# Moving the row statistics of x1 from VectorE to ScalarE and GpSimd, with a new order of one step, in a cross-attention and feed-forward kernel

## The chip, the cores and the metric

The kernel runs on one core of a Trainium2 chip. The metric is the device time of one execution in microseconds (us). A core has five engines that run their own instruction queues in order and meet only through semaphores: TensorE (PE; PEld is its weight loading), VectorE (DVE), ScalarE (ACT), GpSimd (POOL), and SyncE (SP), which here only issues transfers.

## What is computed

For 64 blocks x[b] of 256 rows by 256, each with a context of 120 rows by 192:

```
x  = x + softmax(q kT / sqrt(32)) v @ Wo + bo      q = layernorm(x) @ Wq, k = ctx @ Wk, v = ctx @ Wv, 8 heads
h  = layernorm(layernorm(x), g1, b1)               (x is now x1)
h  = quant(h) @ ternary(w1) + b1                   256 -> 1024
h  = quant(layernorm(gelu(h), g2, b2))
x  = x + h @ ternary(w2) + b2                      1024 -> 256
```

`quant` scales each row by 127 / max|row| and rounds. The two layernorms in front of w1 are folded into one: with mean m and variance v of a row of x1, h = (x1 - m) * g1 * r + b1, with r = (v * (1 + eps) + eps^2) ^ -0.5.

## The kernel before

The work has two stages. In the first, the attention of all 64 blocks runs as a software pipeline; its result x1 and the quantised rows `hq` of the feed-forward input are made there too. In the second, the feed-forward runs over the 64 blocks. The change lies in the first stage.

One step i of the first stage is the function `attn(i, n)`, which each engine has in a version of its own; its order is written out by hand. Steps 28 to 58 run in a hardware loop unrolled by 4; those before and after are written out. In step i, block i has its scores and exponentials, block i-1 its values and sums, block i-2 its output projection and x1, block i-3 its quantisation, block i+2 its queries and keys, and block i+4 the statistics of x. The names that matter:

- TensorE (L1340): `scores` (raw scores, matmul L1249), `values` (o, L1276), `sums` (L1285), two tiles of `project` (y, L1331), `turn_minima` between them (L1256), `first_values`, `shift` (adds the negated maximum to the scores, L1262), `keys` (L1300 to L1305), `queries` (L1321), `spread_inverses` (L1312).
- VectorE (L692), in this order: `affine` of h (i-3; L700), `largest` (maximum of the scores, into nm_part; L689), h_max (L711), nm_row (L716), h_cl (L721), nm_t (L727), addition of x1 (L733), h_qs (L737), inv_sum (L742), bn_stats of x1 (L747), inv_part (L755), bn_aggr (L760), centring of h (L765) with f_ve between its two halves (L769), q_t (L777), o_t (L786). `shift` waits for nm_t, inv_part for ScalarE's inv_hi.
- ScalarE (L1005): copies of keys and values (L1001, L1003), of o (`copy_o`, L984), the statistics of x by two sums and two squares (L1016, L1020), two exponentials (L995), inv_hi (L989), two more exponentials, `cast_rows` (L979).
- GpSimd (L514): add_b2 (i-3), add_bo (i-1), the r chain of block i+3 (three small operations), `quantise` (i-3), and the power f_r (i-2; L541), which `affine` of the next step needs.
- SP (L384) issues each step's transfers, the store and the reload of r (L378, L416) among them, which it waits for in its queue. Weights are loaded one piece a step from step 4 on; eight steps have a wide weight operation on ScalarE (L970 in steps 12 to 15, L962 in steps 20, 22, 24 and 26), behind the body of the step.

PSUM has 8 banks: bank 0 holds sums and spread, bank 1 o and the turned minima nm_p, bank 2 keys and y, banks 2 and 3 queries and values' projection, banks 4 to 7 the scores. `keys` waits for x1's addition, since that reads y out of bank 2.

## Time and profile before

| | |
|---|---|
| median of 3 runs | 1152.22 us (1152.06 to 1157.33) |
| the profiled execution | 1157.24 us, its span 1155.6 us |
| busy: TensorE, VectorE, ScalarE, GpSimd | 984.1, 1070.7, 815.4, 711.5 us |
| share of the span | 85%, 93%, 71%, 62% |
| granted TensorE clock, mean | 0.98 |
| first stage | to some 660 us, 64 steps |
| second stage | from some 690 us |

Times in the rows count from the span's start. An engine's timeline gives start and length of each instruction; neighbours on one engine may overlap by a little, so that the distance of two starts, not the length, is what an instruction costs its engine. In brackets stands how long the engine stood idle ahead of an instruction, and which one released it.

### The profile page before, as it was taken

What the parts mean: (1) busy time and instruction counts of PE and PEld (TensorE: products, weight loads), DVE (VectorE), ACT (ScalarE), POOL (GpSimd) and SP (SyncE); (2) the same over time, 40 slices, a digit from 0 to 9 for tenths busy, and PEclk for the clock granted to TensorE, in tenths of its full rate; (3) what the DMA queues carried; (4) which work ended last, traced back from release to release, by engine and by line L of the source; (5) the groups of instructions that cost most, each with busy time, mean ns of one, the idle gap of its engine ahead of it and who ended that gap; (6) DMA issues with size and microseconds to landing.
All of it is one profiled execution on the core that took longest, in us unless ns stands there. A gap on an engine that the chain in (4) does not pass through costs nothing.

```text
span 1155.6 us, 29367 instructions
## 1 busy us (share of the span) xinstructions
PE 984.1 (85%) x9649; PEld 655.4 (57%) x9649; DVE 1070.7 (93%) x1711; ACT 815.4 (71%) x2091; POOL 711.5 (62%) x930
## 2 busy tenths in 40 slices
PE   5999998999999999999999767887777777777775
PEld 3666666666666666666666433544444444444444
DVE  2799988999999999999999899999999999999997
ACT  3655565566655566556654476999999999999993
POOL 3355555666555555555556436777777777777776
PEclk8999999999999999999999888999999999999998
DMA  4677956666767667776765301333233333323334
GB/s 142 137 159 161 165 125 159 147 148 146 149 152 148 152 144 156 150 150 141 150 149 122 97 19 23 38 37 37 35 38 36 36 36 36 37 36 36 36 36 72
DMA packets 145430, 114.71 MB, mean 99 GB/s; under 512 B 52536, under 2 KB 135864, under 8 KB 145360
## 3 DMA queue, kind: packets, MB, share of 16 engines
q1 hardware_dynamic: 127776, 96.90, 38.4%
q0 software_dynamic: 16864, 16.26, 11.9%
q8 instruction: 40, 0.66, 0.3%
q10 hardware_dynamic: 720, 0.66, 0.2%
q14 instruction: 30, 0.25, 0.1%
HBM read 71.75 MB, written 33.63 MB: 91 GB/s over the span
## 4 chain that ended last, share of the span: by engine, by line
DVE 43%; issue 25%; PE 21%; DMA 6%; SPq 3%; POOL 1%; DVEq 1%; ACT 1%; POOLq 0%; ACTq 0%
DVE nm_part L689 10%; PE banks L1321 9%; DVE gn_low L813 7%; DVE gn_high L813 7%; DMA r_rows<-x_r 5%; PE banks L1300 3%; DVE xr L733 3%; DVE h L700 3%; DVE o_t L786 2%; PE banks L1331 2%; DVE gn_low L799 2%; DVE gn_high L799 2%; PE banks L1302 1%; DVE h_max L711 1%; DVE g_max L819 1%
## 5 line engine op out<-in xcount | busy, mean ns | idle before, releaser
L995 ACT ACTIVATE probs<-banks 120x512 f32<-120x512 f32 x256 | 138.4, 596 | 110.6 <-PE banks L1262 110.5
L689 DVE TRANSPOSE_TENSOR_REDUCE nm_part<-banks 128x64 f16<-128x2048 f32 x64 | 147.8, 2309 | 3.7 <-PE banks L1249 3.7
L1033 ACT ACTIVATE g_dev<-g,g_sum 128x1024 bf16<-128x1024 f32 x128 | 149.1, 1165 | 0.0
L1038 ACT ACTIVATE g<-banks,h_dq 128x1024 f32<-128x1024 f32 x128 | 142.4, 1130 | 8.1 <-PE banks L1196 8.1
L502 POOL TENSOR_TENSOR xr<-xr,b_bc 128x512 f32<-128x512 f32 x64 | 82.6, 1290 | 102.2 <-DVE h L700 100.4
L1331 PE MATMUL banks<-wo_sb,o_t 128*128 128x256 f32 x512 | 140.8, 398 | 1.1 <-DVE o_t L847 1.0
L1214 PE MATMUL banks<-w_t,g_t 128*128 128x256 bf16 x1008 | 125.3, 279 | 14.5 <-ACT g_t L1071 11.9
L1190 PE MATMUL banks<-w_t,h_t 128*128 128x512 bf16 x512 | 127.7, 394 | 2.0 <-ACT g L1038 1.3
L1321 PE MATMUL banks<-xt,wq_c 128*128 128x256 f32 x512 | 128.3, 393 | 0.0
L1214 PEld LDWEIGHTS banks<-w_t,g_t 128*128 128x128 f16 x1008 | 95.8, 100 | 54.1 <-issue 26.8
L574 POOL TENSOR_TENSOR g_r<-g_ve,neg_half 128x2 f32<-128x2 f32 x64 | 104.5, 1633 | 8.6 <-ACT g_ve L1054 8.6
L541 POOL TENSOR_TENSOR f_r<-f_ve,neg_half 128x2 f32<-128x2 f32 x62 | 49.6, 801 | 92.2 <-DVE f_ve L769 92.2
L497 POOL TENSOR_TENSOR xr<-xr,bo_bc 128x512 f32<-128x512 f32 x64 | 81.1, 1266 | 39.3 <-DMA xr<-in_x 39.1
L1321 PEld LDWEIGHTS banks<-xt,wq_c 128*128 128x128 f32 x512 | 92.5, 190 | 17.9 <-issue 0.2
L1331 PEld LDWEIGHTS banks<-wo_sb,o_t 128*128 128x128 f32 x512 | 86.9, 189 | 21.0 <-issue 14.1
L549 POOL TENSOR_TENSOR g_dq<-g_max,w_out 128x2 f32<-128x2 f32 x64 | 12.6, 197 | 131.0 <-DVE gn_low L813 70.5
L1001 ACT ACTIVATE k_t<-banks 128x256 f32<-128x256 f32 x64 | 24.5, 383 | 91.4 <-DVE q_t L777 91.2
L1208 PE MATMUL banks<-ident_h,gn_low 128*128 128x128 f16 x512 | 40.3, 223 | 51.6 <-POOL gn_low L554 51.6
L799 DVE SCALAR_TENSOR_TENSOR gn_high<-g,g_nm,g_bc 128x1024 f32<-128x1024 f32 x64 | 80.9, 1271 | 0.0
L799 DVE SCALAR_TENSOR_TENSOR gn_low<-g,g_nm,g_bc 128x1024 f32<-128x1024 f32 x64 | 80.9, 1271 | 0.0
L813 DVE SCALAR_TENSOR_TENSOR gn_low<-gn_low,g_r,b2n_bc 128x1024 f32<-128x1024 f32 x64 | 79.2, 1279 | 0.0
L1249 PE MATMUL banks<-q_t,k_t 32*128 32x256 f32 x1024 | 75.0, 407 | 4.9 <-ACT k_t L1001 4.8
(167 smaller groups left out, 2599.2 us busy)
## 6 DMA issues: line engine op xcount, KB each, us to landing
x_in<-in_x SPq DMA_DIRECT2D x64, 256.0 KB, 4.6
xt<-in_x_t SPq DMA_DIRECT2D x64, 256.0 KB, 4.2
xr<-in_x SPq DMA_DIRECT2D x64, 256.0 KB, 5.4
out<-xr SPq DMA_DIRECT2D x64, 256.0 KB, 5.9
out<-res POOLq DMA_DIRECT2D x62, 256.0 KB, 4.4
ctx_t<-in_ctx_t SPq DMA_DIRECT2D x64, 128.0 KB, 3.9
r_bc<-r_rows SPq DMA_DIRECT2D x64, 128.0 KB, 4.6
w_raw<-in_w_t SPq DMA_DIRECT2D x8, 256.0 KB, 5.2
```

Source lines behind the costliest of these rows:

```text
L502: pool.tensor_tensor(xr[:, r, :, :], xr[:, r, :, :], b2_bc[:, :].unsqueeze(1).to_broadcast([P, T, D]), ALU.add).then_inc(b2_done, 1)
L574: pool.tensor_tensor(g_r[:, q, :], g_ve[:, q, :], neg_half[:, 0:T], ALU.pow).then_inc(gr_done, 1)
L689: dve.tensor_reduce(nm_part[:, :, 0:C * RB], blocks_p, AX.X, ALU.max, negate=True, apply_transpose=True).then_inc(max_done, 1)
L799: dve.scalar_tensor_tensor(out=gn[n][:, t, :], in0=g[:, p, t, :], scalar=g_nm[:, p, t:t + 1], in1=g2_bc[:, :], op0=ALU.add, op1=ALU.mult). ...
L813: dve.scalar_tensor_tensor(out=gn[n][:, t, :], in0=gn[n][:, t, :], scalar=g_r[:, p, t:t + 1], in1=b2n_bc[:, :], op0=ALU.mult, op1=ALU.add) ...
L995: act.activation(probs[:, p, j, :, :], sc_p[0:KV, j, :, :], ACT.Exp, scale=SCALE).then_inc(probs_done, 1)
L1033: act.activation(g_dev[:, t, :], g[:, p, t, :], ACT.Square, scale=-float(F), bias=g_sum[:, p, t:t + 1], accum_out=g_ssq[:, p, t:t + 1]).th ...
L1038: act.activation(g[:, p, t, :], u_p[t], ACT.Gelu, scale=h_dq[:, b, t:t + 1], accum_out=g_sum[:, p, t:t + 1]).then_inc(gelu_done, 1)
L1190: pe.matmul(u_p[t][:, cols], h_t[:, b, t * C + c, :], w1_t[:, c, cols], start=(c == 0), stop=False, skip_group_check=True)
L1214: pe.matmul(y[t], turned_rows[:, t, f, :], w2_t[:, f, :], start=(first and f == 0), stop=False, skip_group_check=True)
L1321: last = pe.matmul(q_p[:, m, :], wq_c[:, c, m * P:(m + 1) * P], xt[:, p, c, :], start=(c == 0), stop=(c == C - 1))
L1331: last = pe.matmul(y_p[:, t, :], o_t[:, p, c, t * P:(t + 1) * P], wo_sb[:, c, :], start=(c == 0), stop=(c == C - 1))
```

## The change

- VectorE: `largest` comes first in the step. The centring of h moves one step later (block i-3 in place of i-2) and stands behind `largest`; nm_row and nm_t follow, then `affine`, h_max, the addition of x1, h_cl, h_qs, inv_sum, inv_part, q_t, o_t. bn_stats, bn_aggr and f_ve are gone for the blocks up to 61; the last two keep them.
- ScalarE: `row_statistics(i-2)`, two sums (as means) and two squares, stands at the end of the step; `cast_rows` moves ahead of the statistics of x.
- GpSimd: `scale_rows(i-3)` makes f_ve by two small operations and f_r by the power, first in the step; then the r chain, `quantise`, then add_b2 (behind a wait for inv_part) and add_bo.
- TensorE: y moves to bank 1 (`project` waits for copy_o, `values` for x1's addition of the step before), the turned minima to bank 0 (no wait for copy_o). `keys` no longer waits for x1; its short matmuls come first.
- SP: the output's store one step later and ahead of the r store; the reload of r ahead of the load of xr.

```diff
-        y_p = bank[2].rearrange("p (t n) -> p t n", t=T)
+        y_p = bank[1].rearrange("p (t n) -> p t n", t=T)
-        nmt_p = bank[1][:, 0:P // 2].bitcast(F16)
+        nmt_p = bank[0][:, P:P + P // 2].bitcast(F16)
...
+                def scale_rows(b, m):
+                    after(pool, h_affine, b - 1)
+                    pool.wait_ge(x1_ssq, b * T + T)
+                    pool.tensor_tensor(f_ve[:, m, :], f_ssq[:, m, :], var_mul[:, :], ALU.mult).then_inc(f_ve_done, 1)
+                    pool.wait_ge(f_ve_done, 2 * b + 1)
+                    pool.tensor_tensor(f_ve[:, m, :], f_ve[:, m, :], var_add[:, :], ALU.add).then_inc(f_ve_done, 1)
+                    pool.wait_ge(f_ve_done, 2 * b + 2)
+                    pool.tensor_tensor(f_r[:, m, :], f_ve[:, m, :], neg_half[:, 0:T], ALU.pow).then_inc(f_r_done, 1)
...
-                        pool.wait_ge(h_affine, b + 1)
-                        add_b2(b, (n + 1) % 4)
-                    b = i - 1
-                    if live(b, NB):
-                        add_bo(b, (n + 3) % 4)
+                        scale_rows(b, q)
...
+                    b = i - 3
+                    if live(b, NB):
+                        pool.wait_ge(split_done, i)
+                        add_b2(b, (n + 1) % 4)
+                    b = i - 1
+                    if live(b, NB):
+                        add_bo(b, (n + 3) % 4)
...
+                    if isinstance(i, int) and i == -1:
+                        largest(0)
+                    elif live(i, NB) and not (isinstance(i, int) and i == 0):
+                        largest(i)
+                    b = i - 3
+                    if live(b, NB):
+                        after(dve, hq_cast, b - 3)
+                        dve.wait_ge(x1_ssq, b * T + T)
+                        for t in range(T):
+                            last = dve.scalar_tensor_tensor(out=h[:, r1, t, :], in0=xr[:, r1, t, :],
+                                                            scalar=f_mean[:, q, t:t + 1], in1=g1_bc[:, :],
+                                                            op0=ALU.subtract, op1=ALU.mult)
+                        last.then_inc(h_centred, 1)
...
+                def row_statistics(b, p, r):
+                    after(act, f_ve_done, 2 * b - 2)
+                    after(act, h_centred, b - 1)
+                    act.wait_ge(x1_done, b + 1)
+                    for t in range(T):
+                        act.activation(x1_sq[:, p, t, :], xr[:, r, t, :], ACT.Copy, scale=1.0 / D,
+                                       accum_out=f_mean[:, p, t:t + 1]).then_inc(x1_summed, 1)
+                    for t in range(T):
+                        act.wait_ge(x1_summed, b * T + t + 1)
+                        act.activation(x1_sq[:, p, t, :], xr[:, r, t, :], ACT.Square, scale=-1.0,
+                                       bias=f_mean[:, p, t:t + 1], accum_out=f_ssq[:, p, t:t + 1]).then_inc(x1_ssq, 1)
...
-                    if live(i - 4, NB):
-                        cast_rows(i - 4, n % 4)
+                    if live(i - 2, NB):
+                        row_statistics(i - 2, p, (n + 2) % 4)
...
-                    pe.wait_ge(min_done, b + 1)
+                    after(pe, x1_done, b - 1)
...
-                    after(pe, x1_done, b - 3)
+                    after(pe, k_done, b)
...
-                        pe.wait_ge(q_done, left(b + 4))
-                        pe.wait_ge(k_done, left(b + 4))
+                        pe.wait_ge(o_done, left(b + 2))
                         pe.wait_ge(on_done, b + 1)
```

## Rows read from the trace of the kernel before

**Rows 1.** Windows: stretch; busy PE, PEld, DVE, ACT, POOL; clock, DMA share, GB/s.

```profile
300.00:580.00 280.00, 270.10 (x3014) 192.66 (x3017) 265.82 (x577) 166.11 (x484) 160.73 (x258) 1.00 0.70 149
```

**Rows 2.** Timeline, VectorE, one step: start, length, engine, line, operation.

```profile
443.20 2.31 DVE L689 TRANSPOSE_TENSOR_REDUCE nm_part<-banks 128x64 f16<-128x2048 f32 x1
...
445.43 0.64 DVE L711 TENSOR_REDUCE h_max<-h 128x2 f32<-128x512 f32 x1
...
446.90 0.69 DVE L733 TENSOR_TENSOR xr<-banks,xr 128x512 f32<-128x512 f32 x1
...
447.58 0.94 DVE L742 RECIPROCAL inv_sum<-banks 128x128 f32<-128x128 f32 x1
...
448.43 0.69 DVE L747 BATCH_NORM_STATS2 f_st<-xr 128x6 f32<-128x256 f32 x2
...
449.25 0.35 DVE L755 SCALAR_TENSOR_TENSOR inv_part<-inv_hi,part_sign,inv_sum 128x128 f16<-128x128 f16 x1
...
452.95 2.31 DVE L689 TRANSPOSE_TENSOR_REDUCE nm_part<-banks 128x64 f16<-128x2048 f32 x1
```

**Rows 3.** Timeline of the same step, TensorE and ScalarE.

```profile
441.32 1.15 PE L1249 MATMUL banks<-q_t,k_t 32*128 32x256 f32 x16
...
442.01 0.38 ACT L1001 ACTIVATE k_t<-banks 128x256 f32<-128x256 f32 x1 [1.32 <-DVE q_t L777]
...
443.60 0.60 ACT L984 ACTIVATE o_raw<-banks 128x512 f32<-128x512 f32 x1 [0.92 <-PE banks L1276]
...
444.27 1.13 PE L1331 MATMUL banks<-wo_sb,o_t 128*128 128x256 f32 x4
```

**Rows 4.** Timeline of the first steps, TensorE and VectorE.

```profile
31.95 1.15 PE L1249 MATMUL banks<-q_t,k_t 32*128 32x256 f32 x16
...
33.24 2.32 DVE L689 TRANSPOSE_TENSOR_REDUCE nm_part<-banks 128x64 f16<-128x2048 f32 x1 [0.39 <-PE banks L1249]
...
43.54 1.13 PE L1331 MATMUL banks<-wo_sb,o_t 128*128 128x256 f32 x4
...
44.76 0.29 DVE L716 TENSOR_REDUCE nm_row<-banks 128x32 f16<-128x128 f16 x1 [0.54 <-PE banks L1256]
...
45.16 0.42 DVE L727 TENSOR_TENSOR nm_t<-nm_row,block_sel 128x256 f16<-128x256 f16 x1
```

**Rows 5.** Timeline behind the loop, VectorE.

```profile
680.58 0.48 DVE L877 SCALAR_TENSOR_TENSOR h<-h,f_r,b1n_bc 128x256 f32<-128x256 f32 x1
...
681.49 0.69 DVE L882 TENSOR_REDUCE h_max<-h 128x2 f32<-128x512 f32 x1
```

**Rows 6.** Timeline of step 62, VectorE and ScalarE.

```profile
644.69 0.94 DVE L742 RECIPROCAL inv_sum<-banks 128x128 f32<-128x128 f32 x1
...
645.72 0.31 ACT L989 ACTIVATE inv_hi<-inv_sum 128x128 f16<-128x128 f32 x1 [0.16 <-DVE inv_sum L742]
646.09 1.09 ACT L995 ACTIVATE probs<-banks 120x512 f32<-120x512 f32 x2
```

**Rows 7.** Timeline of step 15, ScalarE and TensorE's weight loads.

```profile
181.41 0.30 ACT L989 ACTIVATE inv_hi<-inv_sum 128x128 f16<-128x128 f32 x1
181.61 1.07 ACT L995 ACTIVATE probs<-banks 120x512 f32<-120x512 f32 x2
...
182.74 0.74 PEld L1249 LDWEIGHTS banks<-q_t,k_t 32*128 32x128 f32 x16 [0.30 <-ACT probs L995]
```

**Rows 8.** Timeline, ScalarE: first and last instruction of one block's statistics of x.

```profile
444.09 0.41 ACT L1016 ACTIVATE x_sq<-x_in 128x256 bf16<-128x256 f32 x1
...
445.78 0.19 ACT L1020 ACTIVATION_READ_ACCUMULATOR x_sq<-x_in,x_sum 128x1 f32 x1
```

**Rows 9.** Groups by line, GpSimd: busy us, mean ns | idle before.

```profile
L541 POOL TENSOR_TENSOR f_r<-f_ve,neg_half 128x2 f32<-128x2 f32 x62 | 49.6, 801 | 92.2 <-DVE f_ve L769 92.2
```

**Rows 10.** Timeline, ScalarE: a weight operation of step 15.

```profile
183.09 1.06 ACT L970 ACTIVATE w_t<-w_raw 128x1024 bf16<-128x1024 f32 x1
```

**Rows 11.** SP's queue, 80 to 190 us: waits in total, times, longest.

```profile
SPq L416 <- DMA r_rows<-x_r: 52.0, 11, 6.7
```

More of the change, by code:

```diff
@@ L536, in attn @@
                         weight_steps[i]()
-                    b = i - 2
+                    b = i - 3
                     if live(b, NB):
-                        after(pool, h_affine, b - 1)
-                        pool.wait_ge(f_ve_done, b + 1)
-                        pool.tensor_tensor(f_r[:, p, :], f_ve[:, p, :], neg_half[:, 0:T], ALU.pow).then_inc(f_r_done, 1)
+                        pool.wait_ge(split_done, i)
[3 more added lines that the diff above has]
+                        add_bo(b, (n + 3) % 4)
                 def store(b, r):
@@ L694, in attn @@
                     r1, r2 = (n + 1) % 4, (n + 2) % 4
+                    if isinstance(i, int) and i == -1:
[3 more added lines that the diff above has]
+                    b = i - 3
+                    if live(b, NB):
+                        after(dve, hq_cast, b - 3)
[5 more added lines that the diff above has]
+                        last.then_inc(h_centred, 1)
+                    b = i
+                    if live(b, NB):
+                        dve.wait_ge(nmt_ps, b + 1)
+                        dve.tensor_reduce(nm_row[:, :], nmt_p.rearrange("p (k r) -> p r k", r=32), AX.X, ALU.min).then_inc(min_done, 1)
+                        after(dve, sc_ps, b)
+                        dve.wait_ge(min_done, b + 1)
+                        dve.tensor_tensor(nm_t[:, :, :], nm_row[:, :].unsqueeze(1).to_broadcast([P, RB, 32]),
+                                          block_sel[:, :].unsqueeze(2).to_broadcast([P, RB, 32]), ALU.mult).then_inc(nmt_done, 1)
                     b = i - 3
@@ L703, in attn @@
                         last.then_inc(h_affine, 1)
-                    if isinstance(i, int) and i == -1:
-                        largest(0)
-                    elif live(i, NB) and not (isinstance(i, int) and i == 0):
-                        largest(i)
                     b = i - 3
@@ L735, in attn @@
                     if live(b, NB):
+                        after(dve, hq_done, b - 1)
+                        dve.wait_ge(h_maxed, b + 1)
+                        dve.tensor_scalar(h_cl[:, q, :], h_max[:, q, :], CLIP, 1.0 / QMAX,
+                                          ALU.max, ALU.mult).then_inc(h_clipped, 1)
                         dve.wait_ge(h_clipped, b + 1)
@@ L742, in attn @@
                         dve.reciprocal(inv_sum[:, q, :], sum_p).then_inc(inv_done, 1)
-                    b = i - 2
-                    if live(b, NB):
-                        dve.wait_ge(x1_done, b + 1)
-                        for t in range(T):
-                            last = dve.bn_stats(f_st[:, p, t, :], xr[:, r2, t, :])
-                        last.then_inc(x1_stats, 1)
                     b = i - 1
@@ L891, in _ @@
                 steps(dve, A0, NB, L0, L1, attn, 4, aside)
+                dve.wait_ge(x1_ssq, (NB - 2) * T)
+                centre_h(NB - 3, 1, [f_mean[:, 1, t:t + 1] for t in range(T)])
                 affine_h(NB - 3, 1)
@@ L899, in _ @@
                 statistics(NB - 2, 2)
-                centre_h(NB - 2, 2)
+                centre_h(NB - 2, 2, [f_mv[:, 0, t, 0:1] for t in range(T)])
                 ffn(0, 0, True)
@@ L906, in _ @@
                 statistics(NB - 1, 3)
-                centre_h(NB - 1, 3)
+                centre_h(NB - 1, 3, [f_mv[:, 1, t, 0:1] for t in range(T)])
                 ffn(2, 2)
```

94 lines of the change are left out of this document (36 added, 58 removed).

## The prediction, made before the changed kernel ran

> **What bounds the kernel now.** Read the sum by stage first: between 300 and 580 us VectorE is busy 265.8 of 280 us, TensorE 270.1, ScalarE 166.1, GpSimd 160.7, at granted clock 1.00 [rows 1]. Two engines are near full, so no share decides; the order of one step does. The timeline of VectorE has one block of attention per 9.75 us: `largest` starts at 443.20 and again at 452.95, and nothing stands idle between [rows 2]. TensorE begins the scores of this step at 441.32 [rows 3], 1.88 us before `largest`: VectorE first finishes `o_t` and then the normalisation's second half, `affine`, of an older block. The loop that closes is `largest` -> transposition of the minima -> second output tile -> addition of x1 -> keys -> queries -> `q_t`, `o_t`, `affine` -> `largest`. TensorE waits in it twice, for the minima and for x1, because y shares bank 2 with the keys. By its idle time (9.9 of 280 us, over 28.7 steps) TensorE alone would need about 9.4 us.
>
> **What is taken away.** From VectorE, for each of 62 blocks: bn_stats (start to next start 448.43 to 449.25, 0.82 us) [rows 2], and with it bn_aggr and f_ve, which together are shorter (by the rows' distances I put all three at 1.2 us; the sum below doesn't use it). y moves to bank 1, so the keys no longer wait for x1. `largest` stands ahead of `affine`. If only this counted, VectorE would fall to some 8.5 us and TensorE's 9.4 would set the step.
>
> **The new chain.** Let the scores of block i start at 0. I follow VectorE's new order to the next scores. A self-wait is a wait of an engine for its own last result.
> - Scores to `largest`: 1.29 (31.95 to 33.24, a place where VectorE was free) [rows 4].
> - `largest`: 2.23 (443.20 to 445.43) [rows 2]. Sum 3.52. The two centring instructions now stand here, 0.40 each by the two `affine` instructions, of the same kind and size (680.58 to 680.98 is one) [rows 5]: 4.32. The transposition is done by then (below).
> - nm_row to nm_t with its self-wait: 0.40 (44.76 to 45.16) [rows 4]: 4.72. nm_t is 0.42 long [rows 4]; a neighbour without a self-wait starts 0.08 to 0.09 before the end (inv_sum, 0.94 long, has its next at 0.85 [rows 2]): 0.34, sum 5.06.
> - `affine` twice, then the self-wait for h_max: 0.91 (680.58 to 681.49) [rows 5]: 5.97.
> - h_max, 0.64 long [rows 2], the same overlap: 0.56, sum 6.53. Adding x1 and h_qs before the reciprocal of the sums: 0.68 (446.90 to 447.58) [rows 2]. h_cl now stands between with a self-wait, 0.20 (0.16 of its own and a gap like those above): 7.41.
> - The reciprocal `inv_sum` to ScalarE's inv_hi: 1.03 (644.69 to 645.72) [rows 6]: 8.44. Nothing of VectorE's lies between `inv_sum` and this any more, and ScalarE has long run its first two exponentials.
> - inv_hi to the third exponential: 0.20 (181.41 to 181.61) [rows 7] or 0.37 (645.72 to 646.09, where ScalarE had waited for `inv_sum` as it will here) [rows 6].
> - Third and fourth exponential to the next scores: 1.13 (181.61 to 182.74), where TensorE is shown to wait for exactly this [rows 7].
>
> Sum: 9.77 to 9.94 us, against 9.75. So the step hardly changes: the exponentials stand in ScalarE's queue behind inv_hi, inv_hi behind `inv_sum`, and `inv_sum` now behind centring and `affine`, which before lay partly on the other side of it. I take 9.86, the middle, since both ends are rows of the same operations: +0.11.
>
> The Trainium skill speaks against three of these terms. Its page "VectorE: DVE Perf Modes", section "The DRAIN you can't avoid", says that the pipe empties between two Vector instructions anyway and that a semaphore between them costs nothing extra. By that the self-waits would vanish and the period would not exceed the old one. The rows here disagree: instructions without such a wait overlap by 0.09 us (inv_sum, as above) [rows 2], and with it 0.40 passes for a nm_row of 0.29 [rows 4].
>
> **Does the rest stay hidden?** ScalarE gains two sums and two squares per block. The same four cost 1.88 us at 444.09 to the last accumulator read's end at 445.97 [rows 8]. They start when the last exponential ends, about 0.15 before the next scores, end at +1.7; the copies of keys and values (0.38 each, overlapping by 0.1) end by 2.4, and copy_o, which starts at +2.28 today (443.60 against 441.32) and takes 0.60 [rows 3], ends at 2.9. `project`'s first tile starts at +2.95 now (444.27) [rows 3] and in the new kernel waits for copy_o, since y takes o's bank. From that tile to nm_row 1.22 us pass (43.54 to 44.76, where only the transposition lies between) [rows 4]: 4.17, against 4.32 on VectorE. Covered, by 0.15 to 0.2 us only. ScalarE's total rises to 8.2 us, under 9.8. GpSimd: two small operations and the power, which takes 0.80 [rows 9]; were all three as long, 2.4 from +1.9, so by 4.3, and `affine` asks for it at 5.06. Its r chain of block i+3 follows, of the same three kinds; SP's r store waits for that, and the reload of r has a whole step before use. add_b2 and add_bo come behind inv_part and run beside q_t, o_t and `largest`; x1's addition asks for add_bo only at 6.5 of the next step. Each covered. TensorE's own work arrives at the scores after 9.4 at the latest, and the other path from inv_hi, over inv_part (0.35 long [rows 2]) and the four short spread matmuls, is shorter than the 1.33 through the exponentials.
>
> **Places where it isn't hidden.** Eight steps (12 to 15, and every second from 20) put a wide weight operation into ScalarE's queue behind the new statistics: 1.06 long [rows 10]. It then stands ahead of copy_o, where the cover was 0.2: up to +1.0 each, 8 us. In steps 80 to 190 us SP stands 52 us for r_rows in eleven steps, up to 6.7 [rows 11], while weights load, and steps are longer than 9.85 already; the later x loads and the output ahead of the r store shift this by -3 to +6. Four of the eight steps fall there and their delay partly lies beside that one. I take +4.5 for both. In the unrolled steps, where a step takes 9.85 today, +0.05 of 20 steps: 1.0. The loop of 31 steps: 31 x 0.11 = 3.4. At the end ScalarE has the statistics (1.88) in front of the first bias copy and lost the cast (0.5) there: +1.4.
>
> Sum: 3.4 + 1.0 + 4.5 + 1.4 = 10.3 us. The profiled execution took 1157.24 (span 1155.6), so its like would take 1167.5. That execution lies 5.0 above the median 1152.22, so the median forecast is 1162.5, +0.9%.
>
> **Rivals.**
> 1. *ScalarE's queue costs more* (chance 0.25): 9.95 in the loop (31 x 0.20 = 6.2), 0.15 in 20 unrolled steps (3), all eight weight steps at full price (8), SP's order +4, tail 1.4: +22.6, 1175. For it: the 0.37 row is the one with ScalarE waiting. Against: one row only.
> 2. *The weight steps cost nothing, since they fall beside the transfers* (0.24): 3.4 + 1.0 + 1.4, 1158 or a little less, within 0.5%. A measurement of this kernel can tell about 0.5% from no change, 1146.5 to 1158.
> 3. *TensorE becomes the bound, faster* (0.18): the place is the semaphore waits and the exponentials' start. If the chain above is shorter than 9.4, the step is TensorE's 9.4: -0.35 x 31 and -0.45 x 25, +4 for the rest, 1134. It decides from 0.4 us: for instance, were the three self-waits free (0.20 + 0.11 + 0.05 to 0.13) and inv_hi read earlier. The rule of the Trainium skill cited above gives this same outcome. Against it: the waits show in rows 4 and 5.
> 4. *The change doesn't take hold*: the last two blocks still use bn_stats, but 62 of 64 change, so no chance of its own.
>
> **How the numbers follow.** Forecast 1162.5 with 1158 to 1169: chance 0.33. Slower still 0.25, same 0.24, faster 0.18. Slower by over 0.5%: 0.33 + 0.25 = 0.58. The range leaves out the lower end of rival 3 and the far end of rival 1: 1143 to 1180.
>
> **What would show it.** Right: VectorE idle ahead of `largest` (for the scores) by 0.5 us or more and ahead of inv_part (for inv_hi) by 0.4 in each step; the scores' weight loads waiting for probs; VectorE's busy time in attention down by about 70 us; ScalarE idle some 1.4 us ahead of inv_hi; steps near 9.86. Wrong: steps near 9.4 with TensorE never waiting (rival 3), or the first output tile waiting for o_raw in each step (ScalarE's cover of 0.2 was gone), or f_r or xr late, which would put GpSimd on the path.

## The result, and the profile after

The changed kernel takes 1199.58 us (median, 1197.96 to 1202.08) beside 1154.49 us for the kernel before on the same chip: ratio 1.040, 95% interval 1.0375 to 1.042. The prediction said 1162.5 and 1143 to 1180. The sign was right, the size far off and outside the range.

The profiled execution took 1198.2 us, its span 1196.4. First the busy times over the whole span, from the page:

```profile
PE 977.5 (82%) x9603; PEld 645.7 (54%) x9649; DVE 1025.4 (86%) x1401; ACT 926.1 (77%) x2587; POOL 731.2 (61%) x1056
```

VectorE fell by 45.3 us and ScalarE rose by 110.7, as meant. Now the same window as [rows 1], with the same columns:

```profile
300.00:580.00 280.00, 251.51 (x2799) 174.06 (x2801) 226.20 (x402) 204.74 (x673) 156.01 (x292) 1.00 0.53 137
```

TensorE is busy for 251.5 of 280 us in place of 270.1, VectorE for 226.2 in place of 265.8, and the DMA share fell from 0.70 to 0.53. The two engines that were near full no longer are, and ScalarE is at 204.7 of 280, so something else sets the step. Nearly the whole loss lies in the first stage: from the first `largest` to the last of the 64 pass 628.3 us before (21.6 to 649.9) and 666.2 after (21.3 to 687.5), +37.9 of the +40.8 in the span; 3.25 are behind the last `largest`.

The view that names the culprit is the waits of SP's own queue, 300 to 620 us (total, times, longest):

```profile
SPq L420 <- DMA r_rows<-x_r: 154.2, 31, 6.8
```

SP stands for five of the some ten microseconds of each step in front of the reload of r (r_bc), until its own store of r (r_rows) has landed, that is, until the semaphore that tells of its end has come. For the kernel before, the same view has two rows:

```profile
SPq L416 <- DMA r_rows<-x_r: 80.7, 33, 3.7
SPq L378 <- POOL x_r L531: 60.8, 33, 4.4
```

The second row is the important one, because it is gone afterwards. Before, SP came to the store early and waited for GpSimd's x_r: it had slack in every step. After, it never waits there; x_r has been ready for some time when SP comes. SP's timeline of one step after the change (issue instructions, start and length):

```profile
478.06 0.37 SPq L386 DMA_DIRECT2D r_rows<-x_r  x1
483.63 0.37 SPq L420 DMA_DIRECT2D r_bc<-r_rows  x1
484.28 0.41 SPq L424 DMA_DIRECT2D xr<-in_x  x1
484.85 1.20 SPq L390 DMA_TRANSPOSE h_t<-hq  x1
486.23 0.45 SPq L400 DMA_DIRECT2D ctx_t<-in_ctx_t  x1
486.77 0.38 SPq L402 DMA_DIRECT2D xt<-in_x_t  x1
487.42 0.38 SPq L406 DMA_DIRECT2D x_in<-in_x  x1
487.99 0.41 SPq L410 DMA_DIRECT2D out<-xr  x1
488.58 0.37 SPq L386 DMA_DIRECT2D r_rows<-x_r  x1
493.87 0.37 SPq L420 DMA_DIRECT2D r_bc<-r_rows  x1
...
499.25 0.37 SPq L386 DMA_DIRECT2D r_rows<-x_r  x1
```

The store is issued at 478.06, its landing lets the reload go at 483.63 (5.6 us), and then seven issues stand in a row until the next store at 488.58 (4.95 us). The next round is 5.3 + 5.4. In these rounds the loop passes no compute engine: SP's queue shows no wait for one. It takes 10.5 to 10.7 us, and everything else follows. The chain of work, followed back through 480 to 503 us, says the same; its first entry is

```profile
478.06 5.55 DMA r_rows<-x_r
```

and the landing of r_rows is on that chain again from 488.58 (5.27) and from 499.25. Its users see it on VectorE's timeline; `q_t` waits for the reload, and `largest` starts 10.15 us apart here:

```profile
487.32 0.69 DVE L776 TENSOR_TENSOR q_t<-banks,r_bc 128x512 f32<-128x512 f32 x1 [1.50 <-DMA r_bc<-r_rows]
...
488.53 2.31 DVE L706 TRANSPOSE_TENSOR_REDUCE nm_part<-banks 128x64 f16<-128x2048 f32 x1
...
498.68 2.32 DVE L706 TRANSPOSE_TENSOR_REDUCE nm_part<-banks 128x64 f16<-128x2048 f32 x1 [0.27 <-PE banks L1266]
```

Earlier, before weights are loaded, the steps are the predicted ones:

```profile
59.73 2.32 DVE L706 TRANSPOSE_TENSOR_REDUCE nm_part<-banks 128x64 f16<-128x2048 f32 x1 [0.57 <-PE banks L1266]
...
69.50 2.32 DVE L706 TRANSPOSE_TENSOR_REDUCE nm_part<-banks 128x64 f16<-128x2048 f32 x1 [0.57 <-PE banks L1266]
```

That is 9.77 us. So the engines' chain and SP's loop are two loops of similar length, and the longer one sets the step.

How far from this was the kernel before? SP's timeline of the step of [rows 2]:

```profile
444.97 0.38 SPq L398 DMA_DIRECT2D x_in<-in_x  x1
447.53 0.36 SPq L378 DMA_DIRECT2D r_rows<-x_r  x1
448.07 0.38 SPq L408 DMA_DIRECT2D xr<-in_x  x1
448.67 0.41 SPq L412 DMA_DIRECT2D out<-xr  x1
451.58 0.35 SPq L416 DMA_DIRECT2D r_bc<-r_rows  x1
...
454.67 0.38 SPq L398 DMA_DIRECT2D x_in<-in_x  x1
```

From store to reload pass 4.05 us, with the load of xr and the output's store issued *while* it lands; from the reload to the end of x_in's issue 3.5. That is a loop of some 7.5 us in a step of 9.75, with 2.2 us of slack, which is the wait for x_r between 445.35 and 447.53. The change moved two issues (1.15 us) out of the landing's shadow, and put a 256 KB store right ahead of the 1 KB one. With the old landing that would have been 4.05 + 5.4 = 9.45 us at most, still hidden under 9.77. But the median landing in 300 to 620 us rose from 4.0 to 5.5 us (the list of DMA issues), and 5.5 with 4.95 to 5.4 of issues makes 10.45 to 10.9. By this sum the loss needed both, the moved issues and the longer landing; what made the landing longer stays open (last section).

### The profile page after: what moved, and what is told of

It is laid out like the page before. It is cut to its first block, busy times and chain, and to the rows that moved or that the text cites. A ratio compares the mean times of both kernels' runs of the same rounds, so it can differ in the third digit from the quotient of the medians.

```text
span 1196.4 us, 29791 instructions
## 1 busy us (share of the span) xinstructions
PE 977.5 (82%) x9603; PEld 645.7 (54%) x9649; DVE 1025.4 (86%) x1401; ACT 926.1 (77%) x2587; POOL 731.2 (61%) x1056
## 4 chain that ended last, share of the span: by engine, by line
DMA 26%; DVE 25%; issue 24%; SPq 16%; PE 4%; POOL 2%; ACT 2%; DVEq 1%; ACTq 0%; POOLq 0%
DMA r_rows<-x_r 24%; DVE gn_low L812 7%; DVE gn_high L812 6%; SPq L390 5%; DVE gn_low L798 2%; SPq L410 2%; DMA r_bc<-r_rows 2%; SPq L400 2%; DVE gn_high L798 2%; SPq L424 2%; SPq L406 2%; DVE nm_part L706 2%; SPq L402 2%; SPq L420 1%; DVE g_max L818 1%
## 5 line engine op out<-in xcount | busy, mean ns | idle before, releaser
L706 DVE TRANSPOSE_TENSOR_REDUCE nm_part<-banks 128x64 f16<-128x2048 f32 x64 | 147.7, 2308 | 11.2 <-PE banks L1266 10.7
L1229 PE MATMUL banks<-w_t,g_t 128*128 128x256 bf16 x1008 | 123.7, 277 | 10.4 <-ACT g_t L1086 7.7
L517 POOL COPY h_dq<-h_cl 128x2 f32<-128x2 f32 (+1 forms) x64 | 13.7, 214 | 185.9 <-DVE h_qs L759 184.8
L1205 PE MATMUL banks<-w_t,h_t 128*128 128x512 bf16 x466 | 117.5, 389 | 6.2 <-ACT bias_st L1074 2.4
L1337 PE MATMUL banks<-xt,wq_c 128*128 128x256 f32 x512 | 121.4, 380 | 0.0
L776 DVE TENSOR_TENSOR q_t<-banks,r_bc 128x512 f32<-128x512 f32 x64 | 44.3, 692 | 80.0 <-DMA r_bc<-r_rows 64.3
L1031 ACT ACTIVATE x_sq<-x_in 128x256 bf16<-128x256 f32 x128 | 52.1, 408 | 67.2 <-DMA x_in<-in_x 64.1
L1346 PEld LDWEIGHTS banks<-wo_sb,o_t 128*128 128x128 f32 x512 | 88.6, 193 | 28.5 <-ACT o_raw L997 13.9
L565 POOL TENSOR_TENSOR g_dq<-g_max,w_out 128x2 f32<-128x2 f32 x64 | 12.1, 189 | 131.2 <-DVE gn_low L812 70.7
L1223 PE MATMUL banks<-ident_h,gn_low 128*128 128x128 f16 x512 | 40.8, 224 | 54.2 <-POOL gn_low L570 54.2
L1266 PE MATMUL banks<-q_t,k_t 32*128 32x256 f32 x1024 | 75.0, 408 | 12.2 <-ACT k_t L1014 4.9
L1002 ACT ACTIVATE inv_hi<-inv_sum 128x128 f16<-128x128 f32 x64 | 19.8, 309 | 80.9 <-DVE inv_sum L764 80.7
```

Source lines behind the costliest of these rows:

```text
L706: dve.tensor_reduce(nm_part[:, :, 0:C * RB], blocks_p, AX.X, ALU.max, negate=True, apply_transpose=True).then_inc(max_done, 1)
L1205: pe.matmul(u_p[t][:, cols], h_t[:, b, t * C + c, :], w1_t[:, c, cols], start=(c == 0), stop=False, skip_group_check=True)
L1229: pe.matmul(y[t], turned_rows[:, t, f, :], w2_t[:, f, :], start=(first and f == 0), stop=False, skip_group_check=True)
L1337: last = pe.matmul(q_p[:, m, :], wq_c[:, c, m * P:(m + 1) * P], xt[:, p, c, :], start=(c == 0), stop=(c == C - 1))
L1346: last = pe.matmul(y_p[:, t, :], o_t[:, p, c, t * P:(t + 1) * P], wo_sb[:, c, :], start=(c == 0), stop=(c == C - 1))
```

## The experiments

**Theory A**: SP's loop (landing plus the issues behind the reload) sets the step; beneath it lies the engines' chain of 9.77 to 9.94 that the prediction worked out. **Theory B**: the engines' new order itself costs more, through ScalarE or VectorE, and SP's waiting is only a follower. Ratios are to the kernel before, timed beside each. "In the loop" are the steps from 28 on, of the profiled execution; each profile has some longer steps besides.

| kernel | ratio, 95% interval | span | steps (starts of `largest`) |
|---|---|---|---|
| changed | 1.040 [1.0375, 1.042] | 1196.4 | 9.78 to 11.6 in the loop, mean 10.5 |
| e1, store of r ahead of output | 1.0228 [1.0191, 1.0264] | 1180.5 | 9.77 to 11.1 in the loop, one of 12.2, mean 10.2 |
| e2, reload one step later | 1.017 [1.0147, 1.0192] | 1168.9 | 9.78 and 9.89 in the loop, and two of 11.6 and 12.3 |
| e8, issues behind the store | 1.016 [1.0101, 1.0219] | 1178.5 | 9.78 to 9.92 in the loop, one of 10.1 |
| e3, old engines, SP's new order | 1.0695 [1.0666, 1.0724] | 1227.0 | 10.3 to 12.0 in the loop, mean 11.1 |
| e5, old kernel, reload later | 0.9997 [0.9981, 1.0013] | 1156.2 | 9.75 in the loop, one of 10.4 |
| e4, e2 + inv_sum early | 0.9876 [0.9842, 0.9911] | 1133.2 | 8.9 to 9.2 in the loop, outliers of 9.8 to 12.3 |
| e6, e4 + xr's load later | 0.9782 [0.9751, 0.9812] | 1122.3 | 8.90 to 9.17 in the loop, fewer outliers, 9.5 to 10.5 |
| e7, inv_sum early, SP as changed | 1.0432 [1.0386, 1.0479] | 1212.4 | 9.5 to 12.1 in the loop |
| e10, old kernel, inv_sum early | 1.0316 [1.029, 1.0342] | 1187.6 | 10.38 in the loop |
| e9, e2 + high half last | 1.0064 [1.0038, 1.009] | 1177.4 | 9.59, 9.60, 9.93, 9.72 in turn, and outliers |
| e11, e2 + weight op earlier | 1.0191 [1.0163, 1.0219] | 1168.6 | 10.6 in the weight steps |
| e12, e2 + weight op last | 1.0162 [1.0136, 1.0188] | 1165.8 | 9.78 and 10.47 in the weight steps |

### SP's loop: four ways to shorten it

**e1** stores r ahead of the output:

```diff
-                    b, r = i - 4, n
-                    if live(b, NB):
-                        sp.wait_ge(b2_done, b + 1)
-                        sp.dma_start(out[b]...
                     (store_r of block i+3)
+                    b, r = i - 4, n
+                    if live(b, NB):
+                        sp.wait_ge(b2_done, b + 1)
+                        sp.dma_start(out[b]...
```

> Edit: the changed kernel with the store of r ahead of the output's store on SP's queue, nothing else. Theory A (the step is set by SP's own loop: store of r, its landing, reload, five more issues, next store; 5.3 us landing + 5.4 us issues = some 10.6): one issue (0.55 us) leaves the loop and the landing shortens towards the 4.1 us of the kernel before, so 4.8 + 4.3 = 9.1 to 9.6, under the 9.77 to 9.94 of the engines' chain; steps near 9.85, 1160 to 1172 us in all. Theory B (the extra work on ScalarE and GpSimd holds the step, through late x_in, xr and r): the order of two stores matters little, 1190 to 1200.

Measured 1181.17 us, ratio 1.0228: 18 us less, between the two theories' numbers. SP's waits, 300 to 600 us:

```profile
SPq L420 <- DMA r_rows<-x_r: 113.2, 29, 4.7
SPq L424 <- DMA out<-xr: 23.1, 24, 1.6
```

One issue now runs in the landing's shadow and SP waits 3.9 us a step there in place of 5.0. But the landing still takes 5.3 us (median), though no 256 KB store stands right ahead of it any more, and a new wait has come behind it: xr's load overwrites the buffer of the block four before, needs that block's output landed, and this output has only just been issued. 18 us are 0.3 us per step, less than the 0.6 of the issue that was moved.

**e2** takes the wait out: the reload of block i+2 in step i, ahead of the store of block i+3, so that a whole step lies between a store and its reload.

```diff
+                    b = i + 2
+                    if live(b, NB):
+                        sp.wait_ge(r_stored[p], (b - p) * 8 + 16)
+                        sp.dma_start(r_bc[:, p, :], r_rows[b]...
                     (store_r of block i+3)
-                    b = i + 3
-                    if live(b, NB):
-                        sp.wait_ge(r_stored[q], (b - q) * 8 + 16)
-                        sp.dma_start(r_bc[:, q, :], r_rows[b]...
```

> Edit: the changed kernel with the reload of r issued one step later on SP's queue (block i+2 in place of i+3, ahead of the store of r), so that SP never stands waiting for a store it has just issued. Theory A: SP's loop is gone, what is left is the chain over inv_sum, inv_hi and the exponentials: steps 9.77 to 9.94, 1155 to 1166 us in all; waits of q_t for r_bc and of x_sq for x_in disappear. Theory B (ScalarE's and GpSimd's new work holds the step): 1190 or more.

Measured 1172.38 us (1.017). 27 of the 37 us by which the prediction had missed are back, and nothing but SP's order was touched. Now the timeline of the step shows the chain of the prediction on all engines:

```profile
486.80 1.15 PE L1266 MATMUL banks<-q_t,k_t 32*128 32x256 f32 x16
...
488.09 2.32 DVE L706 TRANSPOSE_TENSOR_REDUCE nm_part<-banks 128x64 f16<-128x2048 f32 x1 [0.57 <-PE banks L1266]
489.75 0.73 PEld L1346 LDWEIGHTS banks<-wo_sb,o_t 128*128 128x128 f32 x4 [0.20 <-ACT o_raw L997]
...
491.08 0.28 DVE L728 TENSOR_REDUCE nm_row<-banks 128x32 f16<-128x128 f16 x1
491.47 0.42 DVE L731 TENSOR_TENSOR nm_t<-nm_row,block_sel 128x256 f16<-128x256 f16 x1
...
494.20 0.95 DVE L764 RECIPROCAL inv_sum<-banks 128x128 f32<-128x128 f32 x1
495.25 0.31 ACT L1002 ACTIVATE inv_hi<-inv_sum 128x128 f16<-128x128 f32 x1 [1.43 <-DVE inv_sum L764]
495.46 1.07 ACT L1008 ACTIVATE probs<-banks 120x512 f32<-120x512 f32 x2
495.66 0.35 DVE L769 SCALAR_TENSOR_TENSOR inv_part<-inv_hi,part_sign,inv_sum 128x128 f16<-128x128 f16 x1 [0.51 <-ACT inv_hi L1002]
...
496.59 0.74 PEld L1266 LDWEIGHTS banks<-q_t,k_t 32*128 32x128 f32 x16 [0.30 <-ACT probs L1008]
```

Scores to `largest` 1.29 (predicted 1.29); scores to inv_sum 7.40 (7.41); inv_sum to inv_hi 1.05 (1.03); inv_hi to the exponentials 0.21 (0.20 or 0.37); to the next scores 1.13 (1.13). In all 9.79 (9.77 to 9.94). Four steps of the loop take 9.78, 9.79, 9.89 and 9.90 in turn, 9.84 in the mean.

**e8** keeps the reload in the same step but gives it a shadow: the store is the first thing in SP's step, then turn, ctx, xt, x_in and out, then the reload. (In the diff, the six lines of `store_r` move from behind the output's store to the top of `attn`.)

> The changed kernel with the store of r as the first thing of SyncE's step (ahead of turn, ctx, xt, x_in and out) and the reload behind them, in the same step. Theory A (the landing of 5.3 us and the 5.4 us of issues stand in a row): the issues now run while the store lands, SyncE's loop falls to about 6 us plus the issues left behind the reload, the engines' chain of 9.8 us takes over: 1165 to 1176 us, near the run with the reload a step later (1172). Theory B (the landing itself is long because of the bulk behind it on the same queue, and grows to 7 to 8 us when four transfers are issued right behind the store): little comes, 1185 to 1198 us.

Measured 1180.59 us, ratio 1.016 (the kernel before took 1158.48 beside it), the same as e2 within the intervals. SP's waits, 300 to 600 us:

```profile
SPq L424 <- DMA out<-xr: 104.1, 30, 4.9
SPq L420 <- DMA r_rows<-x_r: 21.3, 23, 2.2
SPq L386 <- POOL x_r L545: 6.6, 7, 1.7
```

The wait for the landing is down from 5 us a step to 0.7. SP now stands 3.5 us a step at xr's load, for the output that it issued moments before, and in the loop this costs nothing: the steps there are those of e2. SP's waits together (132 us in 300) are not far from what they were (143 in the same 300), while the time fell by 2.3%: how long a queue waits says nothing by itself; which issues stand between its waits does. Theory B's landing of 7 to 8 us behind which the bulk stands isn't borne out: its median is 5.0.

**e5** is the control, the same later reload in the kernel before.

> The kernel before, with its reload of r a step later on SyncE and nothing else. Control for what the later reload gives by itself. Theory A: the kernel before is bound by the engines' chain of 9.75 us in its loop and SyncE's waits there (3.7 us for the landing, 3.0 for r) lie beside it; the edit moves it by under 0.5% in the loop and at most by a few us in the weight steps, 1144 to 1155 us. Theory B (SyncE's waits cost the kernel before as well): about 15 us or more come off, 1138 us or less.

Measured 1158.37 us beside 1158.48, 0.9997 [0.9981, 1.0013]. SP's wait for the landing is gone, its wait for x_r longer:

```profile
SPq L378 <- POOL x_r L531: 92.6, 31, 3.7
```

and the steps are 9.75. SP had slack before, as its row of waiting for x_r said. So the 2.3% that the later reload gives are a matter of the changed kernel alone.

**e3** puts SP's new order into the kernel before: output one step later and ahead of the store of r, reload ahead of xr's load, nothing else.

> Edit: the kernel before with SP's new order alone (output's store one step later and ahead of the store of r, reload of r ahead of the load of xr); all other engines as before. Theory A (SP's loop alone is the price): steps of 10.3 to 10.6 where they were 9.75, 1180 to 1200 us. Theory B (the order on SP is harmless with the old statistics): 1150 to 1158.

Measured 1232.03 us (1.0695), outside both theories' ranges and slower than the changed kernel itself, by another loop than theory A had named. SP still waits for x_r at nearly each store (28 times, 81.4 us), so a loop through GpSimd is the one that is late. GpSimd's timeline:

```profile
485.51 1.27 POOL L497 TENSOR_TENSOR xr<-xr,bo_bc 128x512 f32<-128x512 f32 x1 [5.10 <-DMA xr<-in_x]
```

In the old order of GpSimd, add_bo stands ahead of the r chain. So the loop is store of r, landing, reload, load of xr *behind* it, add_bo, the r chain, store of r. By the rows from 480.35 to 491.38 it takes 0.6 from the reload's issue to that of xr, 4.5 until add_bo, 3.1 until the store of r, and 2.8 until the next reload: 11.0 us, and the mean step of the loop is 11.1. The changed kernel avoids this one, since its GpSimd has the r chain ahead of add_bo. My expectation for this run had missed that in the same way in which the prediction missed SP's loop: a wait in a queue delays all that is issued behind it.

### Behind SP's loop: ScalarE's queue

**e9** is e2 with ScalarE's high half behind all four exponentials:

```diff
-                    if live(i - 1, NB):
-                        high_half(i - 1, q)
                     if live(i, NB):
                         exponentials(i, p, range(HC // 2, HC))
+                    if live(i - 1, NB):
+                        high_half(i - 1, q)
```

> The kernel with the reload a step later (1172 us, steps 9.78 to 9.89), with ScalarE's high half put behind all four exponentials in place of between the second and the third. Theory A (the chain of the step passes ScalarE's high half, 1.43 us of waiting for inv_sum and 0.31 of work, and then exponentials 3 and 4 ahead of the next scores): the scores no longer wait for inv_sum, steps fall to 9.4 to 9.6, 1158 to 1166 us; the transpose of probabilities gets its factors some 1 us later, which could cost a part of it. Theory B (the loop closes over the weight loads that wait for inv_part, not over the exponentials): inv_part comes later by the two exponentials (1.07), steps grow to 10.0 or over, 1180 us or more.

Measured 1166.86 us, 1.0064 against e2's 1.017. (The profiled execution, with a span of 1177.4, is the longest of this kernel's and has single steps of up to 13.9 us; only the steps between them are read.) One of them:

```profile
448.26 2.31 DVE L706 TRANSPOSE_TENSOR_REDUCE nm_part<-banks 128x64 f16<-128x2048 f32 x1
...
457.85 2.32 DVE L706 TRANSPOSE_TENSOR_REDUCE nm_part<-banks 128x64 f16<-128x2048 f32 x1 [0.39 <-PE banks L1266]
```

So the chain did pass through the exponentials behind inv_hi, as predicted, but only 0.19 us of this step hung on it, and 0.13 in the mean of four (9.71 in place of 9.84). The next path is that close, and it is the one over inv_part: in such steps TensorE's weight load of the spread, ahead of the scores, waits 0.84 us for inv_part, and the scores wait for nothing behind it.

**e4** goes to the root, which is where inv_sum stands on VectorE. It is e2 with inv_sum moved from behind h_qs to right behind nm_t:

```diff
                                           block_sel[:, :]..., ALU.mult).then_inc(nmt_done, 1)
+                    b = i - 1
+                    if live(b, NB):
+                        after(dve, split_done, b - 1)
+                        dve.wait_ge(sum_ps, b + 1)
+                        dve.reciprocal(inv_sum[:, q, :], sum_p).then_inc(inv_done, 1)
                     (affine, h_max, x1, h_cl, h_qs)
-                    b = i - 1
-                    ... the same five lines
```

> Edit: as the kernel with the reload one step later, and VectorE takes the reciprocal of the sums right behind nm_t, ahead of affine, h_max, x1 and the quantisation's scale. Theory A (without SP's loop the chain scores, largest, centring, affine, inv_sum, inv_hi, exponentials, scores sets the step at 9.77 to 9.94): inv_hi comes 2.4 us earlier, the exponentials no longer hold the scores, TensorE's own 9.3 to 9.4 us set the step, 1125 to 1142 us. Rival (the step is set by something else on VectorE, its sum or y's addition): no gain over the kernel with the reload later, 1155 to 1166.

Measured 1136.73 us, 0.9876: faster than both kernels, with steps of 8.9 to 9.2. ScalarE no longer waits for inv_sum. Some steps of 10 to 12 us remain, and SP's waits (300 to 600 us) point to them:

```profile
SPq L424 <- DMA out<-xr: 36.3, 21, 5.2
```

**e6** therefore takes that wait out as well: xr's load one step later (block i-1, behind x_in), so that the output it waits for was issued a step ago.

```diff
+                    b, r = i - 1, (n + 3) % 4
+                    if live(b, NB):
+                        after(sp, x1_stored[r], (b - r) * 4)
+                        sp.dma_start(xr[:, r, :, :], x[b]...
                     (out, reload of r, store of r)
-                    b, r = i, n % 4
-                    ... the same three lines
```

> The kernel that beat both (reload of r a step later, inv_sum ahead on VectorE, 1137 us) with the load of xr a step later too, behind x_in and ahead of the output's store, so that SyncE no longer stands on the landing of an output it has just sent. Theory A (the steps of 10 to 12 us between those of 8.98 are SyncE standing on that landing, 36 us of waiting in 300 to 600 us, with r_rows and r_bc behind it): the outliers go, about 1120 to 1130 us, and the wait for out's landing falls under 10 us in that stretch. Theory B (they come from the transfers themselves, 8 us for one landing, whoever waits): no gain, 1133 to 1141 us.

Measured 1126.69 us, 0.9782 [0.9751, 0.9812]. The best version found. In 300 to 600 us SP waits for no output at all, for the reload 0.4 us in total. Its window, columns as in [rows 1]:

```profile
300.00:580.00 280.00, 275.23 (x3191) 201.06 (x3188) 254.75 (x456) 228.00 (x760) 181.34 (x335) 1.00 0.55 158
```

TensorE is busy for 275.2 of 280 us, and in the step from 447.63 to 456.61 (two starts of `largest`, 8.98 us) without a gap: now it is the bound.

Two controls say when moving inv_sum helps. **e7** is the same move with SP as in the changed kernel.

> The changed kernel with VectorE's inv_sum moved up behind nm_t, SyncE's order left as changed. Theory A (SyncE's own loop, store of r, its landing of about 5.3 us, and 5.4 us of issues behind the reload, sets the step): little comes, since the loop of SyncE does not pass VectorE; steps stay at 10 to 10.7 us, 1180 to 1198 us in all, and SyncE still waits over 100 us for the landing of r_rows at the reload. Theory B (VectorE's order sets the step, SyncE's wait is only a follower): the same 36 us come that the move brought with the reload a step later, about 1160 us.

Measured 1210.4 us (1158.48 for the kernel before beside it), 1.0432 [1.0386, 1.0479], beside 1.040 without the move: no gain, though the time lies above theory A's 1198. SP waits as in the changed kernel,

```profile
SPq L420 <- DMA r_rows<-x_r: 143.0, 28, 7.5
```

and VectorE passes the time won on to `q_t`, where it waits for r_bc 54.4 us in 300 to 600 (26 times). Whether the move gives its 36 us hangs on which loop is the longest. **e10** is the move in the kernel before.

> The kernel before with VectorE's inv_sum right behind nm_t and nothing else. Control for whether the gain of 36 us from that move needs the change. Theory A (the loop of the kernel before closes over largest, transposed maxima, keys, queries, q_t, o_t and affine; inv_sum is work in that queue wherever it stands, and ScalarE's high half has slack): the same time within 0.5%, 1149 to 1160 us, steps 9.75 in the loop. Theory B (the exponentials behind ScalarE's high half hold back the scores before as well): 1140 us or less.

Measured 1189.43 us, 1.0316 [1.029, 1.0342]. Neither theory had that: it is slower by 36 us. TensorE's weight loads of `keys` show why:

```profile
487.97 0.52 PEld L1300 LDWEIGHTS banks<-ctx_t,w_kv 128*128 128x128 f32 x4 [1.00 <-DVE xr L738]
```

In the kernel before, this wait is 0.37 us. In both, `keys` takes the bank of y and waits for x1's addition, and inv_sum, 0.95 long, now stands ahead of that addition; the step grows from 9.75 to 10.38, by the 0.63 that `keys` waits longer. So this move is worth -3% on top of e2 and +3% on top of the kernel before. That the new banks are what makes the difference is read from this wait; no run changes the banks alone. By itself the change made no use of the room that it gives to this move.

### The weight steps

In e2, steps 18 to 26 take 10.27 and 10.50 us, not 9.79. GpSimd's timeline in one of them, and then VectorE's:

```profile
241.64 1.04 POOL L482 TENSOR_SCALAR w_raw<-w_raw 128x1024 f32<-128x1024 f32 x1
```

```profile
241.77 1.05 DVE L769 SCALAR_TENSOR_TENSOR inv_part<-inv_hi,part_sign,inv_sum 128x128 f16<-128x128 f16 x1 [0.51 <-ACT inv_hi L1002]
```

inv_part takes 1.05 us in place of 0.35: it ends just behind GpSimd's wide weight operation. **e11** moves that operation ahead of the quantising:

```diff
+                    if isinstance(i, int) and i in weight_steps:
+                        weight_steps[i]()
                     b = i - 3
                     if live(b, NB):
                         quantise(b, (n + 1) % 4)
-                    if isinstance(i, int) and i in weight_steps:
-                        weight_steps[i]()
```

> The kernel with the reload a step later (1172 us), with GpSimd's wide weight operation (1.04 to 1.12 us, steps 18 to 25) put ahead of the quantising and its wait for h_qs, into GpSimd's idle time of 2.7 us. Theory A (beside that operation VectorE's inv_part takes 0.67 to 1.05 us in place of 0.35, and inv_part stands ahead of the spread and the scores on TensorE: steps 10.27 to 10.50 against 9.78): inv_part takes 0.35 in all steps, the eight or nine long steps fall to about 9.8, 4 to 5 us less in all, 1166 to 1169 us. Theory B (those steps are long because of ScalarE's placing and magnitude operations ahead of copy_o, or the transfers of the weights): inv_part falls to 0.35 but the steps stay at 10.2 or over, 1171 to 1174 us.

Measured 1173.6 us, 1.0191 against 1.017: nothing won. inv_part is back at 0.35, but nm_t has been caught instead:

```profile
229.13 1.11 POOL L477 TENSOR_SCALAR w_raw<-w_raw,w_inv 128x1024 f32<-128x1024 f32 x1
```

```profile
229.29 1.23 DVE L731 TENSOR_TENSOR nm_t<-nm_row,block_sel 128x256 f16<-128x256 f16 x1
```

It takes 1.23 in place of 0.42, and this step is 10.59: 9.78 plus just this 0.81. Both theories had inv_part right; neither had foreseen nm_t. **e12** puts it last in GpSimd's step, beside `largest`, which reads PSUM (the two lines go behind `add_bo`).

> The kernel with the reload a step later (1172 us), with GpSimd's wide weight operation behind its last operation of the step (the addition of bo), so that it runs beside largest and the centring. Ahead of the quantising it held nm_t (0.42 to 1.23, steps of 10.60), in its old place inv_part (0.35 to 1.05, steps of 10.27 to 10.50). Theory A (the operation costs by the 16-bit operation of VectorE's path that runs beside it, and no such operation runs beside it here): nm_t 0.42 and inv_part 0.35 in all steps, four or five of the eight long steps fall to 9.8, those with ScalarE's placing operation (every second of steps 20 to 26) keep 0.2 to 0.8 of their own; some 3 us less in the profile of the stretch, 1166 to 1172 us. Theory B (any operation of VectorE beside it is held): largest or the centring takes 0.3 to 1 us more in those steps and they stay at 10.2 or over.

Measured 1170.78 us, 1.0162 [1.0136, 1.0188].

```profile
244.82 2.32 DVE L706 TRANSPOSE_TENSOR_REDUCE nm_part<-banks 128x64 f16<-128x2048 f32 x1 [0.54 <-PE banks L1266]
...
254.61 2.32 DVE L706 TRANSPOSE_TENSOR_REDUCE nm_part<-banks 128x64 f16<-128x2048 f32 x1 [0.57 <-PE banks L1266]
```

`largest` is 2.32 as ever, nm_t and inv_part are 0.42 and 0.35 in all steps, and from step 20 on the steps alternate between 9.78 and 10.47. The long ones are those with ScalarE's placing operation (234.67 and 254.94, 1.05 each) ahead of copy_o: +0.69 where the prediction had "up to +1.0". Theory A's steps, then: 2.2 us less in the eight of them; in the measured time that lies within the intervals. The Trainium skill, page "SBUF — State Buffer", section "Who interferes with whom", says that a Vector instruction with two SBUF inputs contends with a GpSimd instruction that reads SBUF, and calls the port pair that they share an exclusive lock. The rows agree: inv_part and nm_t have two SBUF inputs each and end 0.14 to 0.3 us behind GpSimd's operation, and `largest`, which has none, isn't touched. It doesn't take their 16-bit type, which theory A of e12 had put into its condition. In the kernel before, the centring of h, f32 throughout and with two SBUF inputs, once fell beside the same kind of operation (213.38 to 214.66) and took 1.27 us in place of 0.48:

```profile
213.66 1.27 DVE L765 SCALAR_TENSOR_TENSOR h<-xr,f_mv,g_bc 128x256 f32<-128x256 f32 x1
```

## Why the prediction was right or wrong

**The engines' chain: right.** e2, where nothing else is in the way, has each of the five stretches above within 0.02 us of the prediction's and a step of 9.78 or 9.89; the changed kernel's free steps have 9.77. I had taken 9.86 in the middle, and 9.84 is the mean; the 0.37 us row for ScalarE's turn from inv_hi to the exponentials didn't occur again (0.21).

**The step that failed: SP.** The prediction said of the r chain: "SP's r store waits for that, and the reload of r has a whole step before use. ... Each covered." That weighed when the data is used, not how long SP stands there. In an in-order queue a wait is on the path of all that is issued behind it, the next store included. The sum that was missing could be had from the trace of before: landing 4.05, from the reload to the end of x_in's issue 3.5, and the two moved issues 1.15 make 8.7 us against a step of 9.77. That is a cover of 1.1 us, not "a whole step", and such a cover wants a price. In the changed kernel the issues took 4.95 to 5.4, and the landing 5.5 (median) in place of 4.0, which the trace of before could not tell; but that SP can wait up to 6.7 us for it stood in [rows 11]. The prediction even used that row, at -3 to +6 for eleven steps, as if it belonged to the weights' phase. It was worth 27 us (1199.58 to 1172.38 in e2; 30.6 of the first stage in the profiles, 0.5 a step), and was a rival of its own that the prediction didn't have: SP's own loop becomes the bound.

**The weight steps: mechanism half.** ScalarE's wide operation ahead of copy_o costs 0.69 in e12, as the prediction's mechanism says (cover 0.2, operation 1.05). The other half is GpSimd's operation against inv_part, up to 0.7 of its time, which the prediction didn't have. The kernel before has it too (inv_part 0.81 to 0.84 in those steps), but most of its steps there take 9.98 to 10.01, beside 9.85 in its other unrolled steps, so little hangs on it.

**ScalarE's cover ahead of `project`: right.** "Covered, by 0.15 to 0.2 us only": TensorE's weight load for the first tile waits for o_raw by 0.20 in nearly every step of e2, and `nm_row` still follows the centring without idle time. That row was named as a sign that the forecast would be wrong; it appeared, and cost nothing.

**The end: one term right, others missing.** The prediction had +1.4 for the statistics ahead of the first bias copy. In e2 the chain has the statistics at the place (1.8 us from the last exponential to the copy, where the kernel before has 0.4 for `cast_rows`), and that is +1.4. But from the last `largest` to the end the changed kernel takes 3.25 us more than before and e2 4.7; the rest isn't traced to a cause. The last four steps, which the sum had at nothing, add 3.4 us more in e2: the last takes 12.05 in place of 9.62, and on its chain stands, between the spread and the scores, TensorE's sum of the weights w2 (L1191, 1.7 us).

**TensorE alone at 9.4: too high.** e6 runs steps of 8.98. The 9.4 was TensorE's busy time per step; the same work was busy for 0.4 us less in e6, so busy time was no lower bound. It made rival 3's price too small and hid how much the change could give once inv_sum stands earlier.

**The other signs.** All that "What would show it" listed as right did show in e2: VectorE idle ahead of `largest` 0.57 and of inv_part 0.51, scores' weight loads waiting for probs 0.30, ScalarE idle 1.43 ahead of inv_hi. VectorE's busy time fell by 45, not 70. In the trace of before the lines of bn_stats, bn_aggr and f_ve have 42.7, 14.9 and 10.0 us of their own, but each overlaps its neighbours by up to 0.09, and the total counts an overlap once. Nothing rested on this estimate.

**Without the queue, would the sum have held?** Only in part. The profiles say 13.3 us (spans 1168.9 and 1155.6) where the sum had 10.3, but the profiled execution of the kernel before was a long one. By the medians timed side by side e2 costs 19.5 us (1172.38 and 1152.92), nearly twice the sum. The step was right to 0.1 us; the end and single long steps (11.6 and 12.3 in the loop) were not in the sum.

**The self-waits.** The rule of the Trainium skill, page "VectorE: DVE Perf Modes", section "The DRAIN you can't avoid", that a semaphore between two Vector instructions costs nothing extra would, by the prediction's reading, have given a period of 9.75 or less. In e2, nm_row to nm_t is 0.39 for an nm_row of 0.28, and nm_t, 0.42 long, has its next neighbour, without a wait, after 0.34. The measurement stands by the rows.

## What to carry to other kernels

Treat the queue that issues transfers as an engine: add up its step, each issue and each wait for its own earlier transfer, in order, and compare that with the compute step. A good sign of slack is a wait of that queue for a compute engine; when it is gone after a change, suspect that the queue has become the bound. (In e3 the queue still waited so, and the loop passed through both.) Put a whole step between a store and its reload through DRAM, and remember that one move (inv_sum ahead, here) can be worth -3% or +3% by which loop is the longest.

## What the runs showed of the hardware

- **A 1 KB store took 3.0 to 6.5 us to land in the median, by the order of the queue.** Medians in 300 to 620 us: 3.0 in e3 (nothing issued behind it for 3 us), 3.1 in e6 (the reload 2.2 us ahead, the transposing transfer right behind), 4.0 before, 5.0 in e8, 5.5 in the changed kernel (a 256 KB store 0.6 us ahead), 5.9 in e2 (the load of xr 0.7 us behind), 6.2 in e4 and 6.5 in e9. e2 and e6 have the same two transfers right ahead and differ in what is right behind; e8 (the load of xr 0.6 us ahead) and e6 have the same right behind and differ in what is ahead. So neither side alone accounts for it, and what does, the runs don't separate.
- **Issues aren't free for the issuer.** In the changed kernel 0.33 to 0.45 us each, 1.20 for the transposing one, 0.45 to 0.65 from start to start of the others: seven in a row are 5 us. The Trainium skill, page "DMA: Bandwidth & Descriptors", section "Issuing engines are not separate DMA queues", says that issuing from several engines saves only the time of initiation, which is "usually small relative to the DMA itself". Here one issue is small beside a landing, too, but the seven together were as long as the landing in front of them, and half of the step's bound.
- **A wide GpSimd operation holds VectorE's small operations with two SBUF inputs**: from 0.35 to 1.05 and from 0.42 to 1.23 us for two 16-bit ones, from 0.48 to 1.27 for an f32 one. It leaves the 2.3 us `largest`, which reads PSUM, alone.
